# New tick places for every piece of a fused four-layer kernel on one core

## The reference, cut to what matters

```python
# layer 0: conditioned block
h = silu(scale * layer_norm(x over both axes) + shift) @ W_in + b_in
x = silu(scale * layer_norm(h over both axes) + shift) @ W_out + b_out + x
# layer 1: 16 heads of width 16, bias fside[b, head, 256, 256], key mask
x = ln(x) * (1 + s) + t
q, k, v = x @ Wq + bq, x @ Wk + bk, x @ Wv + bv
x = x + softmax(mask(q k' / 4 + bias)) v @ Wo + bo
x = x + gelu2((ln(x) * g2 + beta2) @ W1 + b1) @ W2 + b2      # 256 -> 1024 -> 256
# layer 2: stencil, first and second differences with coefficient grids
x = max(x + dt * (-gradv(A x) + 0.5 * gradvv(B x)), 0)
# layer 3: causal attention and 256 -> 1024 -> 256, mixed in by a gate
y = x + causal_attention(ln(x)) @ Wo + bo
y = y + gelu(ln(y) @ W1 + b1) @ W2 + b2
out = x + gate * (y - x)
```

## Time and profile before

| | us |
|---|---|
| median of 3 runs | 2771.59 (2771.02 to 2775.16) |
| the profiled execution's own time | 2773.34 |
| its span, first to last instruction | 2772.0 |
| PE busy | 2635.3 (95%) |
| ACT busy | 2351.1 (85%) |
| DVE busy | 2271.4 (82%) |
| POOL busy | 1696.8 (61%) |

### The profile page before, as it was taken

The page is one execution under the profiler, slowest core; times in us unless marked ns, Lnnn a source line. Parts: engine busy times, 40 slices in busy tenths (PEclk is TensorE's granted clock), DMA queues, the critical chain, the costliest instruction groups (busy, mean ns, idle before and its releaser), DMA issues.

```text
span 2772.0 us, 62627 instructions
## 1 busy us (share of the span) xinstructions
PE 2635.3 (95%) x20072; PEld 2219.3 (80%) x20072; DVE 2271.4 (82%) x7925; ACT 2351.1 (85%) x5285; POOL 1696.8 (61%) x1742
## 2 busy tenths in 40 slices
PE   7878999999999999999999999999999999999998
PEld 7766888888888888888888888888888888888776
DVE  5668888888888888888888888888889888888853
ACT  1667889989889899888898988989988898998875
POOL 3665666665666665666666566666566666656431
PEclk8999999999999999999999999999999999999998
DMA  6433333333333333333333333333333333333211
GB/s 226 133 100 97 101 104 117 114 100 106 99 95 110 112 115 97 107 86 105 115 114 100 105 100 99 107 112 117 99 106 85 105 116 111 109 103 95 73 31 28
DMA packets 176549, 287.96 MB, mean 104 GB/s; under 512 B 45856, under 2 KB 99104, under 8 KB 175840
## 3 DMA queue, kind: packets, MB, share of 16 engines
q1 hardware_dynamic: 176224, 283.97, 34.9%
HBM read 174.64 MB, written 8.45 MB: 66 GB/s over the span
## 4 chain that ended last, share of the span: by engine, by line
PE 49%; DVE 19%; ACT 15%; issue 7%; POOL 5%; SPq 2%; DMA 2%; DVEq 0%; ACTq 0%; POOLq 0%
PE bank L1182 9%; PE bank L1175 9%; PE bank L1203 7%; PE bank L1160 6%; PE bank L1152 6%; DVE PB L790 5%; ACT PB L994 5%; DVE PO L798 4%; PE bank L1195 3%; ACT PH L1000 3%; PE bank L1167 2%; ACT AA L1015 2%; POOL AA L540 2%; DVE sme L893 1%; PE bank L1221 1%
## 5 line engine op out<-in xcount | busy, mean ns | idle before, releaser
L994 ACT ACTIVATE PB<-PB,mx 128x256 f32<-128x256 f32 (+1 forms) x2048 | 842.9, 475 | 20.9 <-DVE mx L790 20.1
L798 DVE TENSOR_TENSOR PO<-bank,PH 128x384 f16<-128x384 f32 (+1 forms) x1024 | 590.3, 617 | 210.9 <-ACT PH L1000 210.1
L1000 ACT ACTIVATE PH<-bank 128x384 f16<-128x384 f32 (+1 forms) x1024 | 505.0, 540 | 106.5 <-PE bank L1203 104.9
L501 POOL TENSOR_TENSOR BT<-BT,MN 128x1024 f32<-128x1024 f32 x256 | 546.1, 2138 | 39.6 <-DMA BT<-in_bias 38.9
L1195 PE MATMUL bank<-Ks,Qs 96*128 96x512 f32 (+1 forms) x1024 | 519.7, 512 | 43.1 <-DVE mx L790 35.5
L1203 PE MATMUL bank<-ident,PB 128*128 128x128 f32 x3584 | 506.5, 278 | 24.2 <-DVE PO L798 17.3
L1203 PEld LDWEIGHTS bank<-ident,PB 128*128 128x128 f32 x3584 | 415.8, 143 | 90.8 <-ACT PB L994 40.0
L790 DVE CUSTOM_DVE_ANT_0 PB<-bank,BT 128x256 f32<-128x256 f32 x1024 | 388.6, 417 | 60.3 <-PE bank L1195 58.1
L790 DVE CUSTOM_DVE_ANT_0 PB<-bank,caus 128x128 f32<-128x128 f32 (+1 forms) x1024 | 320.5, 352 | 44.0 <-PE bank L1195 43.8
L1221 PEld LDWEIGHTS bank<-VP,PH 128*128 128x128 f16 x3584 | 205.4, 96 | 111.5 <-issue 104.9
L1175 PE MATMUL bank<-TN,Wf 128*128 128x256 f32 x1024 | 252.0, 389 | 16.8 <-ACT BB L1015 10.4
(11 more groups left out here) (225 smaller groups left out, 5446.6 us busy)
## 6 DMA issues: line engine op xcount, KB each, us to landing
BT<-in_bias SPq DMA_DIRECT2D x256, 512.0 KB, 3.9
Qs<-QH SPq DMA_DIRECT2D x512, 64.0 KB, 2.1
Ks<-KH SPq DMA_DIRECT2D x1024, 32.0 KB, 2.0
Qs<-QU SPq DMA_DIRECT2D x256, 64.0 KB, 2.1
Ks<-KU SPq DMA_DIRECT2D x512, 32.0 KB, 2.0
XT<-in_xT SPq DMA_DIRECT2D x32, 256.0 KB, 4.2
X<-in_x SPq DMA_DIRECT2D x32, 256.0 KB, 2.9
AB<-ada_rows SPq DMA_DIRECT2D x32, 256.0 KB, 3.4
```

The costliest lines, as they stand in the source:

```text
L501: G.op.tensor_tensor(v2(BT[k % 4]), v2(BT[k % 4]), MN[:, :].unsqueeze(1).broadcast_to([128, 2, 512]), ALU.add).then_inc(g_bt, 1)
L798: V.op.tensor_tensor(PO[i][:, 0:w], bP[h][:, 0:w], PH[i][:, 0:w], ALU.subtract).then_inc(v_low, 1)
L994: S.op.activation(o, o, ACT.Exp, scale=-1.0, bias=mx[u.layer][:, c:c + 1]).then_inc(a_exp, 1)
L1000: S.op.activation(PH[i][:, 0:w], bP[h][:, 0:w], ACT.Copy).then_inc(a_high, 1)
```

## The change

Only the numbers of the tables `P` and `OWN` change, in all of them. No instruction, wait, buffer or DMA is added or removed, and all engines keep the same number of instructions. The places of the units' own pieces on PE, DVE and ACT (`score`, `bias`, `exp`, `flip`, `high`, `low`, `pv`, `pvn`) stay as they are in `P`; for the first matrices `OWN` changes them too. The core of the diff:

```diff
 P = {
     "score0": -2, "score1": 0, "bias0": 1, "bias1": 3, "exp0": 3, "exp1": 6, "flip0": 7, "flip1": 7,
     "high0": 8, "high1": 8, "low0": 10, "low1": 10, "pv0": 12, "pv1": 12, "pvn": 15,
-    "ld_bt": -8, "mask_add": -4, "stack": -7,
-    "ld_x": -104, "ld_xn": -44, "ld_ab": -26, "ld_mask": -103, "mask": -28,
-
-    "n1_stats": -91, "n1_ones": -67, "n1_sum": -65, "n1_center": -65, "n1_rstd": -65, "n1_scale": -61,
-    "n1_tanh": -59, "n1_gate": -57, "win": -45, "win_out": -42,
-    "n2_stats": -41, "n2_ones": -40, "n2_sum": -35, "n2_center": -35, "n2_rstd": -32, "n2_scale": -32,
-    "n2_tanh": -30, "n2_gate": -30, "xb": -30, "wout": -29, "x1": -28, "x1_rstd": -26, "x1_norm": -26,
-    "ada": -25, "t1": -24, "t1_out": -21, "x1_bo": -20, "q1": -19, "q1_out": -17, "q1_lo": -12,
-    "k1": -17, "k1_out": -13, "k1_lo": -8, "v1": -13, "v1_out": -7, "v1_hi": -4, "v1_sub": 6, "v1_mid": 9,
+    "ld_bt": -14, "mask_add": -9, "stack": -10,
+    "ld_x": -103, "ld_xn": -34, "ld_ab": -34, "ld_mask": -109, "mask": -25,
+
+    "n1_stats": -81, "n1_ones": -68, "n1_sum": -66, "n1_center": -65, "n1_rstd": -66, "n1_scale": -60,
+    "n1_tanh": -58, "n1_gate": -56, "win": -49, "win_out": -45,
+    "n2_stats": -39, "n2_ones": -39, "n2_sum": -38, "n2_center": -36, "n2_rstd": -36, "n2_scale": -34,
+    "n2_tanh": -31, "n2_gate": -31, "xb": -33, "wout": -30, "x1": -28, "x1_rstd": -25, "x1_norm": -25,
+    "ada": -23, "t1": -21, "t1_out": -20, "x1_bo": -3, "q1": -19, "q1_out": -17, "q1_lo": -13,
+    "k1": -17, "k1_out": -13, "k1_lo": -10, "v1": -13, "v1_out": -9, "v1_hi": -5, "v1_sub": 7, "v1_mid": 8,
     "v1_lo": 10,
 
-    "c1": 44, "c1_out": 45, "o1": 45, "m1": 47, "m1_rstd": 48, "m1_norm": 52, "m1_b": 64, "t2": 54, "t2_out": 54,
+    "c1": 44, "c1_out": 45, "o1": 45, "m1": 47, "m1_rstd": 47, "m1_norm": 53, "m1_b": 71, "t2": 54, "t2_out": 54,
     "w1": 57, "w1_out": 58, "w1_gelu": 66, "w2": 68, "f1": 74,
-    "s_pm": 74, "s_b": 76, "s_r": 74, "s_rp": 76, "s_re": 88, "s_ha": 82, "s_w": 88, "s_ab": 91, "s_row": 92,
+    "s_pm": 74, "s_b": 82, "s_r": 74, "s_rp": 79, "s_re": 91, "s_ha": 83, "s_w": 91, "s_ab": 92, "s_row": 92,
     "s_mm": 95, "s_f": 104,
 
-    "ld_w1": -28, "ld_sten": -41, "ld_w3": -191, "coefs": -20,
-
-    "film_a": -91, "film": -65, "adas": -59, "scr": -58,
-
-    "m3": -40, "m3_rstd": -39, "m3_norm": -35, "t3": -34, "t3_out": -34, "y3": -32, "q3": -30, "q3_out": -26,
-    "q3_lo": -24, "k3": -25, "k3_out": -23, "k3_lo": -17, "v3": -22, "v3_out": -21, "v3_hi": -15, "v3_sub": 2,
-    "v3_mid": 4, "v3_lo": 7, "c3": 43, "c3_out": 44, "o3": 44, "m4": 47, "m4_rstd": 48, "m4_norm": 52, "m4_b": 67,
-    "t4": 53, "t4_out": 54, "w3": 55, "w3_out": 57, "w3_gelu": 66, "w4": 68, "out": 76, "st_out": 85,
+    "ld_w1": -24, "ld_sten": -46, "ld_w3": -277, "coefs": -21,
+
+    "film_a": -72, "film": -62, "adas": -57, "scr": -48,
+
+    "m3": -41, "m3_rstd": -41, "m3_norm": -35, "t3": -34, "t3_out": -33, "y3": -25, "q3": -30, "q3_out": -25,
+    "q3_lo": -24, "k3": -25, "k3_out": -24, "k3_lo": -14, "v3": -22, "v3_out": -19, "v3_hi": -4, "v3_sub": 1,
+    "v3_mid": 9, "v3_lo": 10, "c3": 45, "c3_out": 45, "o3": 46, "m4": 49, "m4_rstd": 50, "m4_norm": 52, "m4_b": 65,
+    "t4": 53, "t4_out": 54, "w3": 55, "w3_out": 57, "w3_gelu": 67, "w4": 69, "out": 75, "st_out": 77,
 }
...
 OWN = {
...
     0: {
-        "score0_1": -6, "score1_1": -3, "bias0_1": -3, "bias1_1": -3, "exp0_1": 0, "exp1_1": 0, "flip0_1": 1,
-        "flip1_1": 1, "high0_1": 1, "high1_1": 2, "low0_1": 2, "low1_1": 2, "pv0_1": 5, "pv1_1": 6, "pvn_1": 8,
-        "ld_bt_1": -3, "mask_add_1": -3, "stack_1": 0, "stack_3": -9, "ld_x": -253, "ld_xn": -36, "ld_ab": -49,
...
+        "score0_1": 5, "score1_1": 7, "bias0_1": 7, "bias1_1": 9, "exp0_1": 10, "exp1_1": 11, "flip0_1": 11,
+        "flip1_1": 11, "high0_1": 13, "high1_1": 14, "low0_1": 14, "low1_1": 14, "pv0_1": 15, "pv1_1": 16,
+        "pvn_1": 18, "ld_bt_1": -2, "mask_add_1": 7, "stack_1": 5, "ld_x": -343, "ld_xn": -75, "ld_ab": -31,
...
```

More of the change, by code:

```diff
@@ L92 @@
     -2: {
[7 rows of a table removed]
[7 rows of a table added]
     },
     -1: {
[4 rows of a table removed]
-        "s_b": 89, "s_r": 90, "s_rp": 90, "s_re": 93, "s_ha": 90, "s_w": 93, "s_ab": 94, "s_row": 95, "s_f": 99,
[4 rows of a table removed]
-        "st_out": 1129,
-    },
[11 rows of a table removed]
-        "w1_gelu": 68, "w2": 70, "f1": 77, "s_pm": 82, "s_b": 93, "s_r": 83, "s_rp": 94, "s_re": 97, "s_ha": 96,
-        "s_w": 98, "s_ab": 98, "s_row": 98, "s_mm": 102, "s_f": 102, "m3": -55, "m3_rstd": -54, "m3_norm": -52,
[3 rows of a table removed]
-    },
[4 rows of a table removed]
-        "stack_3": -4, "ld_x": -116, "ld_xn": -91, "ld_ab": -33, "ld_mask": -68, "mask": -37, "n1_ones": -70,
[6 rows of a table removed]
-        "w1_out": 62, "w1_gelu": 68, "w2": 69, "f1": 75, "s_pm": 75, "s_r": 78, "s_rp": 79, "s_ha": 98, "s_w": 98,
[3 rows of a table removed]
[4 rows of a table added]
+        "s_b": 91, "s_r": 85, "s_rp": 86, "s_ha": 93, "s_w": 93, "s_ab": 93, "s_row": 93, "s_f": 98, "m3": -54,
[4 rows of a table added]
+    },
[11 rows of a table added]
+        "s_b": 88, "s_r": 88, "s_rp": 90, "s_re": 95, "s_ha": 95, "s_w": 96, "s_ab": 97, "s_row": 98, "s_mm": 100,
[3 rows of a table added]
+    },
+    1: {
+        "score0_1": 1, "score1_1": 3, "bias0_1": 3, "exp0_1": 6, "flip0_1": 11, "flip1_1": 11, "high0_1": 12,
+        "high1_1": 12, "low0_1": 14, "low0_3": 9, "low1_1": 14, "pv0_1": 15, "pv1_1": 15, "pvn_1": 18, "ld_bt_1": -16,
+        "mask_add_1": 1, "stack_1": -13, "stack_3": -9, "ld_x": -72, "ld_xn": -57, "ld_ab": -28, "ld_mask": -62,
[6 rows of a table added]
+        "s_r": 80, "s_rp": 88, "s_ha": 97, "s_w": 100, "s_ab": 101, "s_row": 106, "s_mm": 106, "s_f": 108,
+        "m3_rstd": -35, "y3": 0, "q3_lo": -25, "k3_out": -23, "k3_lo": -7, "v3_hi": -19, "v3_sub": -18, "v3_mid": -14,
+        "v3_lo": -10, "m4_b": 71, "out": 77,
     },
```

## The result

The changed kernel takes 2741.14 us (median of 4 runs, 2738.30 to 2744.39), the one before 2771.31 beside it (2769.36 to 2775.16): a ratio of 0.989, 95% interval 0.9873 to 0.9907. The profiled execution took 2738.30, 35.0 less than that of before (2773.34). In the changed file all lines behind the tables are numbered four lower: L1195 is L1191 now, L1167 L1163, L1160 L1156, L893 L889.

The account below looks back on a forecast made before the run. PE was taken to set the pace, 97% busy, with only 137 us of idle time to win. 28 periods x 0.6 us = 17 us less than 2773.3 profiled gave 2756 us; range 2730 to 2798.

Parts of the forecast that it names:

- B: Rival: POOL's work does not collide with DVE's stencil, DVE keeps its 2.0 us; 1.6 us a period, 2727 us; chance 0.15.
- A: The forecast: POOL's work over DVE's stencil costs 1.6 of 2.0 us; 0.6 us a period won, 2756 us; chance 0.43.
- c3, o3, win and m4: Start of the period: PE's 1.08 us wait for DVE becomes some 1.5 of smaller waits, yet PE is 0.55 us ahead.
- s_re's 1.93 us: DVE's s_re products: the 1.93 us lost to POOL's mask additions goes, since those now end before s_re begins.
- What POOL does now: POOL's xb, v3_sub and m4_b follow n2_sum and run over DVE's stencil; DVE loses 1.6 us, bounds 0 and 5.1.
- C: Rival: POOL gets every turn between s_re and s_ab, DVE loses 3.5 us; 2808 us, or 2790 with one turn less; chance 0.28.
- Up to wout: DVE's stretch from s_ab to n2_gate, then PE's wout and flip 7: done at 1629.2, before 1629.8; 0.6 us a period won.
- The rest of the period: From 1629.8 to the next 1599: PE has only 0.4 us idle, nothing more won; cost 0, between -0.4 and +0.5.
- SP: SP's queue: the stack starts later, behind ld_bt 7, and lands just as score0 6 is due; price 0, up to 0.5 a period.
- The signs: Expected in the profile after: smaller DVE wait, new ACT waits of 15 us or more, s_re without mask additions, POOL's wait 2 us.
- Clock: PE's lower clock in some ten periods: 0.37 us each may go, 3 us, but new waits could bring it back; 0.
- Fill and drain: Start and end of the run: the fill's load chain keeps its length; taken as 0, bounds -8 and +8 us.

Follow-up runs that it names:

- e4: The kernel before with only c3, c3_out, o3, m4, m4_rstd, v3_out, s_rp, win and win_out at their new places: 2795.04 us, ratio 1.0084.
- e1: The changed kernel with ld_xn, the load of X, put back from -34 to -44: 2799.67 us, ratio 1.0098.
- e11: The changed kernel with ld_xn at -37 instead of -34, so only the load of X and s_row change places in SP's queue: 2760.67 us, ratio 0.996.
- v4: The changed kernel with stack and k1_lo one tick earlier, at -11: 2866.96 us, ratio 1.034.
- o_tail: The changed kernel with the tables of the last two matrices as in the kernel before: 2738.20 us, ratio 0.9873.

## Why the prediction was right, and where it was not

*Direction and range: right, the case: wrong.* 2741 is in 2730 to 2798, but the case that happened is B, which had a chance of 0.15, not A with 0.43. That 2756 came out near 2741 is in part luck: the mechanism it rests on did not occur.

*c3, o3, win and m4: right, and nearly in size.* PE's wait for DVE fell from 29.4 us to 0.2. In its place o3 waits 0.45 a period (forecast 0.55) and t4 0.78 (about 1); PE is 0.32 us ahead at t4 (0.55). e4 shows that this size hangs on m4_rstd's place on POOL, which the forecast didn't price: 2.3 us without it. Where I wrote that m4_norm stays near 1608.4 to 1609.5 I had looked at ACT only.

*s_re's 1.93 us: right for its period, too high for the run.* The two products take 0.23 together, and the mask addition of unit 7 ends at 1508.6, 6.6 us before they begin. But "1.93 us in every period before" was not so: L893's 51.5 busy us fell to 7.8 (as L889), 43.7 in 32 matrices, 1.4 each; in eight of the periods the first product took only 0.86 to 1.00 us.

*What POOL does now: the step that failed.* "xb runs from about 1615.9 to 1617.1, just over the begin of s_re." The distance was taken from n2_rstd as if that were xb's only release. xb has two, n2_rstd in POOL's list and the load of X in SP's queue. With ld_xn behind s_row the second is last, 7.42 us later. I had weighed for B that POOL may be late and against it that n2_sum to xb is a fixed distance; the queue was not looked at. The loss taken as 1.6 us was 0. The price of B, 1.6 a period, is near the measured 1.53, though its own times give 1.8 (wout at 1625.4 and, by the same 2.6 us as in A, the end of wout and flip 7 at 1628.0, before 1629.8). Set on the times of rows 4 by flip 1, the changed kernel has s_re at 1616.6 (forecast 1616.1), the end of s_ab at 1620.0 (1619.5) and wout at 1625.9, each about 0.5 later than B has it; hence 1.35 there instead of 1.8.

*C's mechanism: true, and cheaper to reach than forecast.* e1 shows what POOL does once released: DVE loses 2.2 us a matrix, in s_re, both s_ab and the copy, so "no row shows two losses in a row" was no argument. I had the point from which the change loses at 2.2 us of loss a period. e1 at 2.2 is 28 us slower than before, e11 at 0.9 is 11 us faster. A straight line between these two puts the point near 1.3, and at the 1.6 us that case A had it gives 9 us slower, not 17 faster. That is an estimate from two runs, and no run lost 1.6, but it makes it likely that the gain of A was mis-sized as well.

*Up to wout:* wout is free of n2_gate, as B has it, and PE's own work sets the third. *The rest of the period:* 0.13 of gain, forecast 0. *SP:* score0 6 waits 0.24 us in some periods, 2.7 us in all, inside 0 to 0.5. v4 shows that the cover above it is no slack: a tick earlier costs 126 us.

*The signs:* four came as given (PE's wait for DVE under 10 us, no mask addition beside the s_re products, L925 unchanged at 684 ns, 80.0 for B against 80.20), and two roughly: the wait for ACT's TC is 12.7 us where 15 or more stood, and POOL waits 2.77 us for n2_sum where 2 stood.

*Clock:* the granted clock of the 28 periods rose from 0.99 to 1.00. Before, 9 of 25 periods stand at 0.98, after, 1. Such a period is 0.37 us longer, so this is 8 x 0.37 = 3 us, the size given and then set against an equal loss that didn't come. It is so little because DVE led: in the period of the earlier trace rows win is 1.37 us longer (3.26, not 1.89) and t4 comes 13.01 us behind flip 1 instead of 11.33, but the first s_re products, held until the mask additions end, then take 1.06 us and not 2.17, and the score behind wout comes 31.35 us behind flip 1 instead of 31.07.

*Fill and drain:* 5.5 us lost in the fill and nothing in the drain's tables (o_tail), inside the 8 us. What lost them in the fill is open. PE was busy 3.3 us longer there (210.07, before 206.74) at the lower granted clock (0.88, before 0.93), so the clock is a candidate that no run separates.

*What was read wrongly from the start:* that only 137 us of idle time could be won. It stayed at 138; the gain sits in waits that the busy time covers, and in win's matmuls at the lower clock.

## What to carry to other kernels

When a piece is moved, list all its releases, its own load among them, and follow that load through its DMA queue to what is waiting in front of it: a load behind a DMA that waits for an engine is tied to that engine's progress, and that can shield or starve a third one. Parts of an order don't add (here three parts were 42 and 24 us slower and 15 faster alone, and the whole change is 30 faster), so a part's effect can only be measured on the rest that it was made for. And read PE by the distances of its anchors from version to version, since idle time that is cut into pieces under 0.2 us stands as busy.

## What the runs showed of the hardware

A DVE instruction of one partition and 256 elements (L924) is held until POOL's 128x512 addition has ended, 1.35 us instead of 0.27 (e11). The addition is stretched too, from 1.27 to 1.70: it began 0.56 us before the end of DVE's addition L922 (1524.84 against 1525.40). Back-to-back additions on DVE do not keep POOL out: in e1 the two s_ab of 0.68 took 1.17 each (medians 1175 and 1168 ns), while v3_sub's two of 0.67 took 1.90 together in the period shown. In these rows each side gives way in turn, and both lose.
